# Cross-attention with a routed feed-forward layer: transposed output weights loaded in halves, split of the output weights in reverse order, centroids' bank read before the last exponentials

## What is computed

```python
lat  = layer_norm(_layernorm(x), ln_l_g, ln_l_b);  c = layer_norm(ctx, ln_m_g, ln_m_b)
q    = lat @ Wq                                       # 16 heads of 64
k, v = split(concatenate([c, lat], axis=1) @ Wkv)     # 256 keys per batch
x    = x + (softmax(q @ k.T / 8) @ v) @ Wout          # per batch and head
z    = _layernorm(x)
e    = argmax(z @ centroids.T)                        # one of 8 experts per token
xn   = xhat(z) * ln_g[e] + ln_b[e]
y    = z + relu(xn @ w1[e].T + b1[e]) @ w2[e].T + b2[e]
out  = x + a * y + (1 - a) * z,   a = sigmoid(z @ centroids[e])
```

## Time and profile before

| | us |
|---|---|
| median of 3 runs | 1070.32 |
| lowest, highest | 1070.15, 1070.99 |
| profiled execution | 1066.71 |
| its span | 1064.9 |

### The profile page before, as it was taken

The page is one execution under the profiler, slowest core; times in us unless marked ns, Lnnn a source line. Parts: engine busy times, 40 slices in busy tenths (PEclk is TensorE's granted clock), DMA queues, the critical chain, the costliest instruction groups (busy, mean ns, idle before and its releaser), DMA issues.

```text
span 1064.9 us, 24086 instructions
## 1 busy us (share of the span) xinstructions
PE 1051.3 (99%) x8454; PEld 941.1 (88%) x8454; DVE 796.3 (75%) x1907; ACT 670.9 (63%) x1820; POOL 494.8 (46%) x647
## 2 busy tenths in 40 slices
PE   8989999999999999999999999999999999999998
PEld 6879898988888888989898888888898999999997
DVE  7867888888888988888888888898886554544441
ACT  6765757585676766575757567676555646656551
POOL 2744464646454555546464645455445342222222
PEclk9999999999999999999999999999999999999999
DMA  6576667585757676766658575766367657767670
GB/s 209 120 194 148 165 166 189 139 218 139 207 144 185 150 194 163 188 161 174 181 146 213 145 206 139 190 149 157 90 170 226 236 196 249 240 223 232 227 260 28
DMA packets 159660, 190.51 MB, mean 179 GB/s; under 512 B 17453, under 2 KB 149037, under 8 KB 154672
## 3 DMA queue, kind: packets, MB, share of 16 engines
q1 hardware_dynamic: 155088, 179.09, 61.6%
q0 software_dynamic: 3360, 8.53, 2.2%
q10 hardware_dynamic: 1088, 1.31, 0.4%
HBM read 65.72 MB, written 46.07 MB: 105 GB/s over the span
## 4 chain that ended last, share of the span: by engine, by line
PE 94%; POOL 2%; DVE 2%; DMA 1%; issue 1%; ACT 0%; SPq 0%; POOLq 0%; DVEq 0%
PE psum L698 17%; PE psum L731 16%; PE psum L873 12%; PE psum L768 11%; PE psum L858 10%; PE psum L747 9%; PE psum L783 9%; PE psum L717 8%; PE psum L786 1%; POOL prob L1701 1%; POOL w_o_lo L1758 0%; DVE neg_max L1307 0%; DMA prob_t<-r_ring 0%; POOL r_ring L1701 0%; DMA c_in<-in_ctx_in 0%
## 5 line engine op out<-in xcount | busy, mean ns | idle before, releaser
L1701 POOL TENSOR_TENSOR prob<-prob,inv_sum 128x512 f32<-128x512 f32 x172 | 179.4, 1057 | 195.9 <-DVE inv_sum L1313 195.5
L1307 DVE TENSOR_REDUCE neg_max<-psum 128x2 f32<-128x512 f32 x256 | 162.2, 673 | 36.8 <-PE psum L747 36.8
L1052 ACT ACTIVATE prob<-psum,neg_max 128x256 f32<-128x256 f32 x344 | 160.4, 479 | 32.3 <-DVE neg_max L1307 31.7
L873 PE MATMUL psum<-w,v_n 128*128 128x256 f32 x608 | 134.2, 379 | 0.0
L1319 DVE STREAM_TRANSPOSE prob<-prob 128x512 f32<-128x512 f32 x172 | 118.5, 699 | 12.1 <-POOL prob L1701 11.7
L873 PEld LDWEIGHTS psum<-w,v_n 128*128 128x128 f32 x608 | 114.2, 190 | 14.8
L1701 POOL TENSOR_TENSOR w_ring<-w_ring,inv_sum 128x512 f32<-128x512 f32 x76 | 78.2, 1042 | 79.8 <-DVE inv_sum L1313 79.8
L1059 ACT ACTIVATE head_out_hi<-psum 128x512 fp32r<-128x512 f32 x52 | 31.0, 597 | 118.8 <-PE psum L768 103.0
L1775 POOL DMA_INDIRECT out<-x_in,r_ring x38 | 39.6, 1043 | 130.3 <-DVE x_in L1551 129.6
L1038 ACT ACTIVATE v_n<-psum 128x512 f32<-128x512 f32 x128 | 77.9, 609 | 27.4 <-PE psum L731 22.6
L1027 ACT ACTIVATE k_hi<-psum 128x512 fp32r<-128x512 f32 x128 | 77.1, 603 | 19.1 <-PE psum L698 17.8
(11 more groups left out here) (189 smaller groups left out, 2712.1 us busy)
## 6 DMA issues: line engine op xcount, KB each, us to landing
sorted_rows<-filler SPq DMA_DIRECT2D x54, 660.0 KB, 5.0
prob_t<-prob SPq DMA_DIRECT2D x172, 128.0 KB, 2.8
w_ring<-prob SPq DMA_DIRECT2D x172, 128.0 KB
w<-in_experts SPq DMA_DIRECT2D x19, 1024.0 KB
w_ring<-in_experts SPq DMA_DIRECT2D x18, 1024.0 KB, 5.9
prob_t<-w_ring SPq DMA_DIRECT2D x76, 128.0 KB, 2.8
w_ring<-w_ring SPq DMA_DIRECT2D x76, 128.0 KB
w_ring<-normed SPq DMA_DIRECT2D x56, 128.0 KB, 3.0
```

The costliest lines, as they stand in the source:

```text
L873: last = pe.matmul(bank[:, 0:d_model], hid[:, s % 2, f, i * P:(i + 1) * P], w2[:, f * d_model:(f + 1) * d_model], start=(f == 0), stop=(f ...
L1052: act.activation(prob_at(u, bb)[:, :, parity, i], scores_i, ACT.Exp, bias=neg_max[:, at, i:i + 1], accum_out=prob_sum[:, at, i:i + 1]).the ...
L1307: dve.tensor_reduce(neg_max[:, (4 * u + n) % 8, :], psum[:, n, :].rearrange("p (i j) -> p i j", i=2), AXIS_X, ALU.max, negate=True).then_i ...
L1701: pool.tensor_tensor(probs, probs, inverse, ALU.mult).then_inc(s_soft, 1)
```

## The change

`load_w_out_t` is called once for each half: half 0 in SyncE's second step, behind the moves of that step's first half, with the wait for the weight pieces; half 1 in its third step, behind the moves of the second step's second half, with a wait for two pieces (four of eight increments) of the split. GpSimd splits the pieces from the rear to the front. On ScalarE `high_centroids` comes ahead of the last exponentials of the fifth step, on VectorE `low_centroids` ahead of the last inverse sums of that step.

```diff
--- before.py
+++ after.py
@@ -539,11 +539,14 @@
                         wait_made(sp, ("wout", 2 * g - 1))
                     sp.dma_start(x_cols[:], x_t[:, 2 * g:2 * g + 2]).then_inc(s_xt, 16)
 
-                def load_w_out_t():
-                    sp.wait_ge(s_wlo, len(pieces))
-                    sp.wait_ge(s_wo_split, 2 * W_OUT_PIECES)
-                    for h in range(2):
-                        sp.dma_start(w_o_t[h], w_out_t[:, :, h * half:(h + 1) * half]).then_inc(s_wo_t, 16)
+                def load_w_out_t(h):
+
+
+                    if h == 0:
+                        sp.wait_ge(s_wlo, len(pieces))
+                    else:
+                        sp.wait_ge(s_wo_split, W_OUT_PIECES)
+                    sp.dma_start(w_o_t[h], w_out_t[:, :, h * half:(h + 1) * half]).then_inc(s_wo_t, 16)
 
                 def scattered(end):
 
@@ -589,6 +592,8 @@
                         move_inputs(g + 1)
                     if u > 0:
                         move_probabilities(u - 1, 1)
+                    if u == 2:
+                        load_w_out_t(1)
                     if u == n_steps - 4:
                         sp.wait_ge(s_table, 1)
                         scattered(early_batches)
@@ -609,8 +614,8 @@
                         fill_rows(u - 3)
                     if u < n_steps:
                         move_probabilities(u, 0)
-                    if u == 2:
-                        load_w_out_t()
+                    if u == 1:
+                        load_w_out_t(0)
                     if (u == 1 or u >= 4 and r == 0) and g + 2 < n_pairs:
                         load_pair(g + 2)
                     if r == 3 and g < n_pairs:
@@ -1199,11 +1204,11 @@
                         high_weights(V_REST)
                     if following:
                         high_queries(u + 1)
+                    if u == 4:
+                        high_centroids()
                     exponentials(u, 3)
                     if u == 0:
                         read_values(0, 1, 1)
-                    if u == 4:
-                        high_centroids()
                     if r == 3 and g >= 1:
                         gate_of(2 * g - 2)
                     if r == 0 and g >= 2:
@@ -1614,9 +1619,9 @@
                     inverse_sums(u, 2)
                     if following:
                         low_queries(u + 1)
-                    inverse_sums(u, 3)
                     if u == 4:
                         low_centroids()
+                    inverse_sums(u, 3)
                     if u == 0:
                         low_weights(V_REST)
                     if r in (1, 2) and 1 <= g < n_pairs - 2:
@@ -1748,7 +1753,8 @@
 
                 def split_w_out(i):
 
-                    chunks = slice(i * HC // W_OUT_PIECES, (i + 1) * HC // W_OUT_PIECES)
+                    at = W_OUT_PIECES - 1 - i
+                    chunks = slice(at * HC // W_OUT_PIECES, (at + 1) * HC // W_OUT_PIECES)
                     if i == 0:
                         pool.wait_ge(s_wo, 16)
                     hi, lo = [w[:, chunks, 0:d_model] for w in w_o]
```

## The result

The changed kernel takes 1064.14 us (median of 4 runs, 1063.76 to 1064.63), the kernel before on the same chip 1070.36 us (4 runs, 1070.15 to 1070.99): a ratio of 0.995, interval 0.9938 to 0.9962. The two profiled executions differ by 2.5 us only (1066.71 and 1064.21). So the trace moved as forecast, and the timed runs moved by more than twice as much.

What follows compares the result with a forecast made beforehand. The prediction took PE, with work in 99% of the span, as the bound, so time could come only from its waits. It summed 2.37 + 0.4 = 2.8 us, from 1070.32 to 1067.5 us, range 1066.8 to 1069.0.

Steps and rivals of the forecast that it cites:

- The loads, the moves and the missing wait: SyncE's loads at about 41 and 46 us, moves at 55.4 instead of 57.5, no L768 wait for `r_ring`.
- the wait's 2.37 us: Fourth step's `outputs`: PE's wait for the third step's second half of moves goes entirely, gaining 2.37 us.
- the centroids' 0.4: Fifth step's `outputs`: the centroids' bank is freed earlier, gaining 0.34 to 0.44 us, taken as 0.4.
- The rival of the second step's moves: Wait moves to the second step's moves, behind the first half load: about 1069.0 us, chance 0.15.
- its middle price: Second step's moves landing in 4.24 us, between 2.7 and 5.4: at 49.8, before PE wants them at 50.85.
- The 2.7 us that it gives to the last of four moves: Third step's second-half moves, no load before them: last goes out at 57.26, lands 2.7 us later at 59.96.
- its margin of 1.5 us: Fourth step's `outputs`: moves land at 59.96, PE asks for this half at 61.49, margin 1.5 us.
- A landing of 6 to 7 us: Second step's moves: so slow a landing brings back 0.8 to 1.8 us, about 1069.0 us in all.
- Pricing the wait by starts: Fourth step's `outputs` to scores, start to start: 4.27 us against an undisturbed 1.90, so the wait costs 2.37 us.
- an offset that I leave as it is: Median of the timed runs lies 3.61 us above the profiled execution; kept unchanged in the forecast.
- 3.24 us: The moves' wait of 2.37 us and centroid wait of 0.87 us together, said to be all the edits can reach.
- The rival "it does nothing measurable": Timed runs' waits lie elsewhere than the profiled one's, or a later wait takes the gain: 1070.3 us, chance 0.06.

Runs made afterwards that it cites:

- the loads alone: The changed kernel with the old order of the centroids' bank reads put back on ScalarE and VectorE, keeping half loads and reversed split: 1064.71 us, ratio 0.9958.
- centroids alone: The kernel before with only the earlier read of the centroids' bank, loads and split as before: 1069.39 us, ratio 0.9998.
- split alone: The kernel before with only the order of the four split pieces reversed: 1070.32 us, ratio 1.0003.
- before again: The kernel before, unchanged, run again for its spans and a second trace: 1069.96 us (10 runs); the traced execution took 1069.68 us.
- before, further trace: The kernel before, unchanged, run once more for a further trace: 1069.74 us.
- five products: The kernel before with five unused products of constants on PE between the halves of the fourth step's outputs: 1068.49 us, ratio 0.999.
- nine: The kernel before with nine unused products of constants on PE between the halves of the fourth step's outputs: 1069.86 us, ratio 1.0006.

## Why the prediction was wrong

Its steps on the trace held. The loads, the moves and the missing wait stand where they were put, apart from 0.37 us at the start; the wait's 2.37 us and the centroids' 0.4 (0.43 measured) add up to 2.8; the span is 2.6 shorter, with that later start in it. The rival of the second step's moves came close to its middle price (3.6 us to land) and cost nothing.

Two of its readings were off without harm. The 2.7 us that it gives to the last of four moves is the median of the four, so its margin of 1.5 us was a little smaller. A landing of 6 to 7 us would have brought back 0.7 to 1.7 us, not 0.8 to 1.8. Pricing the wait by starts was right: the idle column has less (2.2 against 2.37), since the records of matmuls are longer here than their cadence. A group of `outputs` lasts 1.97 us in the earlier trace rows, and the scores start 1.90 us after it.

The step that failed is the price of the wait: 2.37 us, from one execution, with the 3.61 us between that execution and the median carried to the end as "an offset that I leave as it is". So 3.24 us was not "all that these edits can reach". The traces of 1069.68 and 1069.74 us show that most of the 3.61 us is no offset. It is the same wait, in executions that pay more for it, and the edit takes that away as well. The sum was made against one execution that was among the fastest of its kind: of 64 runs of before beside the experiments the fastest took 1066.88 us. Sorted by the mean granted clock over the span:

| mean clock | runs of 64 | median us |
|---|---|---|
| 0.999 or 1.0 | 11 | 1067.7 |
| 0.998 | 16 | 1069.6 |
| 0.997 | 20 | 1069.4 |
| 0.996 | 17 | 1071.0 |

The profiled execution of before is of the first row, and so are all 10 runs of the changed kernel and all 5 of the loads alone.

The size, term by term: the wait was put at 2.37 us; in the two traces of a middling execution of before it is 3.5. The clock was not in the sum at all; it costs 1.4 and 1.5 there. With the 0.43 of the centroids that is 5.4 us, against a measured 5.4 in the batch where both kernels ran (1069.24 and 1063.86). That it fits to a tenth is luck, since the two executions are 0.4 to 0.5 us above that batch's median. In the first batch it was 6.2, with four runs of before on its slower side; of an execution of before above 1069.74 us there is no trace, so the last 0.8 us are not shown. Five traces of a kernel with the wait of before:

| execution, us | second half of the weights lands after | last move lands after | clock | more than 6.37 us |
|---|---|---|---|---|
| before, 1066.71 | 5.4 | 4.24 | stays | 2.37 |
| centroids alone, 1067.01 | 6.3 | 4.98 | stays | 3.12 |
| split alone, 1068.77 | 6.4 | 5.16 | stays | 3.32 |
| before again, 1069.68 | 6.6 | 5.37 | falls | 5.04 |
| before, further trace, 1069.74 | 6.7 | 5.40 | falls | 4.93 |

The wait and the clock of the third, whose clock stays:

```profile
65.40 1.09 PE L768 MATMUL psum<-prob_t,v_n 128*64 128x128 f32 x16 [3.09 <-DMA prob_t<-r_ring]
```

```profile
66.00:68.00 2.00, 2.00 (x34) 1.75 (x29) 0.56 (x1) 0.65 (x2) 0.00 (x0) 1.00 0.93 251
```

So both theories hold in part. The longer wait is shown by the traces; the clock is shown by the rows at 0.50, and by the runs that kept PE busy, where it stayed up. How much of the medians is the clock's is less sure: five products brought 0.75 us, nine, too long for the wait, brought nothing. The rival "it does nothing measurable" did ask whether the timed runs have the waits of the profiled one, and then let that speak for less gain only. It can as well mean more.

Not settled: why the same four moves behind 1 MB take 4.24 to 5.40 us to land in different executions (the table shows that the load ahead of them is late too, not what makes it late); why a wait of 3.1 us left the clock alone and one of 3.3 us didn't; and why nine products on PE, with the clock kept, still gave times up to 1071.4 us.
The Trainium skill (TensorE: Matmul & The Clock Gate, section Part 1: The HAM clock gate) describes the two clock levels and says, of a kernel's start, that the number of slow matmuls of one kernel differs from run to run. The table of clocks shows such a spread for a wait in the middle of a kernel: the same program has 0.996 to 1.0.

## What to carry to other kernels

Before a stall is priced from one trace, compare that execution with the timed runs: where what lies around the span is alike, a gap of several us between them is in the span. Here it was for the most part in the very stall that was read, and a second trace, of an execution near the median, shows it. A wait of PE can have a second price, the work at the lower clock; here it showed only in the executions with the longer wait. And a semaphore that counts finished work of several kinds should count it in the order in which it is finished.

## What the runs showed of the hardware

With an idle stretch of 3.3 us on PE the granted clock fell from 1.00 to 0.50 in two traces, once just before the stretch ended and once 1.3 us after, and the work behind took 1.4 and 1.5 us longer; with 2.2, 2.9 and 3.1 us it stayed in three. With 5.1 us it fell inside the stretch, and the work behind took 2.7 us longer; over the span it was 0.997 or less in all 10 runs of that kernel. Work whose results nobody reads kept it up: no run of 23 with such products fell below 0.999.

Four moves of 128 KB took 2.7 us from issue to landing with no load ahead of them and 3.6 us behind 512 KB of weights and 512 KB of inputs (medians of the four). The last of the four took 4.24 to 5.40 us behind 1 MB of weights and 6.11 us behind 1.5 MB.
